# Reordering one slot of a fused attention loop: full-array products first, then both score groups, then values and denominators

## The chip, the cores and the metric

The kernel runs on one Trainium2 chip, the same program on each of its 8 cores, with different tokens on each and nothing exchanged between them. Each core has a matrix engine (TensorE, PE in the profile), a vector engine (VectorE, DVE), an activation engine (ScalarE, ACT), a general engine (GpSimd, POOL) that here only issues DMAs, and SyncE (SP), which issues the other DMAs. Each engine works through its own list of instructions in the order in which the program gives them, and stops at an instruction whose semaphores have not been reached. The metric is the device time of the slowest core in microseconds (us).

## The reference, cut to what matters

One transformer layer over 16 sequences of 2048 tokens with 1024 features; each core takes 2 sequences (4096 tokens).

```python
h = layernorm(x)
Q, K, V = h @ wq, h @ wk, h @ wv             # 16 heads of 64
local  = softmax over a window of 256 keys back (blocks of 256) @ V
remote = latent attention (64 pooled latents, 8 heads) @ r_out_w
gl = sigmoid(Q . gate_local_w); gr = sigmoid(Q . gate_remote_w)     # one number per token and head
x = x + (gl * local + gr * remote) @ w_out
h = layernorm(x)
for blk in range(3):                          # feed-forward, quantised weights with a low-rank part
    y = gelu(layernorm(qlora_linear(h, 2*blk)))
    h = qlora_linear(y, 2*blk + 1) + h
x = x + h
# qlora_linear: h @ ((q / 7.5 - 1) * scale + lb @ la).T + bias
```

## The kernel before, in words

A core's 4096 tokens are 8 tiles of 512 (`NJ = 8`, index `j`); a sequence is 4 tiles (`JS = 4`), so the first tile of a sequence (j = 0 and 4) has no keys behind it and has fewer score blocks. The program has three parts: a latent part (the remote attention, up to about 264 us of the span), the local attention loop (to about 855 us), and the feed-forward part.

The attention loop is software-pipelined over tiles. Of tile j it first computes the values projection and the gate logits, and then goes through 8 slots, p = 0..7, each for one pair of heads, numbered g = 8j + p. A slot holds work of several tiles: the attention of pair g, the k and q projections of tile j+1 (for j = 7, where there is no next tile, the first feed-forward product `y1` stands in their place), the output projection `wout` of tile j-2, and `bcast`, which spreads the softmax and gate factors of the pair of the tile before over the partitions. At p = 1 and 5 a slot also has `lora`, a product of the low-rank part for one chunk of dequantised feed-forward weights.

The products of a slot differ in how they use the 128x128 array. `project`, `wout` and `y1` are 8 matmuls of 128 rows by 128 columns, 512 elements wide (lines 543, 553, 571 and 441). `scores` (line 453) and `bcast` (line 530) work on 64 rows, two at a time. `attend` writes 32 columns, four at a time: values at line 483, denominators at line 496. `lora` (line 514) has 32 rows.

The order is written out by hand, once for each engine. In a slot TensorE does bcast, k, wout, (lora), attend(g), first and second scores of pair g+1, q, third scores of g+1. ScalarE follows the same order: evacuation of k (`k_evac`, line 810), of the attention values (line 960, into `A_O`), `exp_a` and `exp_b` (line 821, 1024 elements each), now and then `centre` (line 846), `exp_p(..., "sc")` (line 821), evacuation of q (line 752). VectorE does `spread` (lines 1159 and 1160, multiplying by the factors that bcast left), `mask_c(g)` (line 1114), `add_sides` (line 1166), `dequant_w` at p = 1 and 5 (lines 1211, 1219, 1230), `resid` on wout's result (line 1178), and `mask_ab(g+1)` (line 1114). For j = 1 `spread` stands behind `mask_c`.

All results pass through PSUM in units that are shared in turn; before a product overwrites a unit it waits until the last content has been read (`u.drained`):

- `S0` (two banks): first scores and third scores. The third scores wait for `exp_a`, the next first scores for the exponential of the third.
- `S1` (two banks): second scores, `bcast` and `lora`. bcast waits for `exp_b`; lora waits for `spread`; the second scores wait for whatever stood there last, at p = 1 and 5 `dequant_w`.
- `UO`, `UD`: attention values and denominators.
- `J[0]`, `J[1]`: k, wout and q (or y1), in turn.

attend(g) also waits for `p_masked`, the mask after the third exponential.

Of the kernel before, what the change touches and what calls it, by code (L numbers as in the profile page):

```python
# [85 lines left out]
def build_program():  # L86
# [38 lines left out]
    with contextlib.ExitStack() as es:  # L125
# [200 lines left out]
        def pe(t):  # L326
# [139 lines left out]
            def scores_b(g):  # L466
                scores(g, S1, "sb", ([(-1, 0, 2, 0)] if (g // 8) % JS else []) + [(2, 2, 2, 256)])

            def scores_c(g):
                scores(g, S0, "sc", [(1, 1, 3, 0), (3, 3, 1, 384)])  # L470
# [194 lines left out]
            for j in range(NJ):  # L665
                for n in range(8):
                    if j >= 1:
                        values(j, n)
                    if n == 3:
                        u = junit["z", j] = nextj()  # L670
                        k = u.take("z", j)
                        t.wait_ge(u.drained, k)
                        if j == 0:
                            for m in (6, 7):
                                w = junit["q", 0, m]
                                t.wait_ge(w.drained, w.nth["q", 0, m])
                        for c in range(8):
                            for side in range(2):
                                for qq in range(4):
                                    mm = t.matmul(u.ap[32 * qq:32 * qq + 32, side * 128:side * 128 + 128],  # L680
                                                  GZ[:, (2 * c + side) * 32:(2 * c + side) * 32 + 32],
                                                  a(A_Q + c * 512 + qq * 128, 128),
                                                  start=(c == 0 and side == 0), stop=(c == 7 and side == 1))
                        mm.then_inc(u.filled)
                if 1 <= j < NJ - 1:
                    t.wait_ge(ld_xt[(j + 1) % 2], 16 * ((j + 1) // 2))
                for p in range(8):
                    g = 8 * j + p
                    if j >= 1:
                        bcast(g - 8)  # L690
                    if j + 1 < NJ:
                        project("k", wk, j + 1, p)
                    else:
                        y1(p // 4, 2 * (p % 4))
                    if j >= 2:
                        wout(j - 2, p)
                    if p in (1, 5):
                        lora(2 * j + p // 4)
                    if p == 0:
                        for n in (6, 7):  # L700
                            u = junit["v", j, n]
                            t.wait_ge(u.drained, u.nth["v", j, n])
                    attend(g)
                    if g + 1 < 8 * NJ:
                        scores_a(g + 1)
                        scores_b(g + 1)
                    if j + 1 < NJ:
                        project("q", wq, j + 1, p)
                    else:
                        y1(p // 4, 2 * (p % 4) + 1)  # L710
                        if p == 5:
                            stats(0)
                    if g + 1 < 8 * NJ:
                        scores_c(g + 1)


            for oc in range(8):
# [31 lines left out]
        def act(s):  # L749
# [73 lines left out]
            def exp_a(g):  # L823
                exp_p(g, S0, "sa", 0, 0)
# [110 lines left out]
            for j in range(NJ):  # L935
# [9 lines left out]
                for p in range(8):  # L945
                    g = 8 * j + p
                    if p % 2 == 0 and 4 * (j - 2) + p // 2 - 1 >= 0:
                        rstd_a(4 * (j - 2) + p // 2 - 1)
                    if j + 1 < NJ:
                        k_evac(j + 1, p)  # L950
                    else:
                        if p == 0:
                            s.wait_ge(cb_done, 1)
                        if p == 6:
                            rstd_b(0)
                        y1_evac(p // 4, 2 * (p % 4))
                    if j >= 1:
                        s.wait_ge(mixed, g - 7)
                    s.wait_ge(UO.filled, UO.nth["av", g])
                    s.activation(a(A_O + p * 512, 512), UO.ap, AF.Identity).then_inc(UO.drained)  # L960
                    if g + 1 < 8 * NJ:
                        exp_a(g + 1)
                        exp_b(g + 1)
                    if p in (2, 6) and j < 4:
                        centre(2 * j + p // 4)
                    if g + 1 < 8 * NJ:
                        exp_p(g + 1, S0, "sc", 1024, 0)
                    if j + 1 < NJ:
                        evac(junit["q", j + 1, p], ("q", j + 1, p), a(A_Q + p * 512, 512))
                    else:  # L970
                        y1_evac(p // 4, 2 * (p % 4) + 1)
                    if j + 1 == NJ and p < 4:
                        square_s(0, 2 * p)
                        square_s(0, 2 * p + 1)
# [713 lines left out]
```

## Time and profile before

| | |
|---|---|
| median of 3 runs | 1600.84 us (1599.74, 1600.84, 1633.67) |
| profiled execution, its own time | 1590.74 us |
| span of its slowest core (core 0) | 1589.2 us |
| PE busy | 1487.5 us, 94% |
| DVE busy | 995.0 us, 63% |
| ACT busy | 878.9 us, 55% |
| attention loop | about 264 to 855 us of the span |

The profiled execution's time is 1.5 us more than its span. All times of the rows are counted from the start of the span of core 0. A row of the timeline gives the start, the length from the first start to the last end, the engine, the line, what is written from what, and how many instructions it merges; in square brackets stands the idle time of the engine just before and what ended it. Matmuls overlap, and their recorded ends are modelled, so distances between starts are what to go by. Where a group of 8 matmuls shows as x7, one record is missing; the row of the weight loads (PEld) has all 8 then.

### The profile page before, as it was taken

The numbers are of one execution on the slowest core, as the hardware profiler recorded it, in microseconds if no ns is written. First come the engines' busy times: TensorE is split into PE (matmuls) and PEld (weight loads), VectorE is DVE, ScalarE is ACT, GpSimd is POOL, SyncE is SP. The second block draws the span as 40 slices with busy tenths as digits, with TensorE's granted clock in tenths as the row PEclk, the third lists the DMA queues.
The fourth block names the chain that finished last, engine by engine and source line by source line (L and its number), as shares of the span: only waits on it lengthen the run. The fifth ranks groups of instructions, "written<-read, shape, count | busy, mean of one in ns | idle before, by whom it ended". The sixth has DMA issues, their size and how long they took to land.

```text
span 1589.2 us, 30285 instructions; the slowest of 8 cores (1573.7 to 1589.2 us)
## 1 busy us (share of the span) xinstructions
PE 1487.5 (94%) x10737; PEld 691.1 (43%) x10906; DVE 995.0 (63%) x1549; ACT 878.9 (55%) x1274; POOL 110.5 (7%) x196
## 2 busy tenths in 40 slices
PE   4797999988999999999998989999999999999997
PEld 2443443444444444444444334444444444444443
DVE  6874313335656565757575766787776767766765
ACT  3575566756555554656576355565556544554552
POOL 3220000000000000000001000011001010000000
PEclk9898999999999999999999999999999999999999
DMA  9999416311223242423756455323122222223323
GB/s 133 178 195 204 99 53 132 93 55 35 78 71 100 68 121 68 115 60 100 143 126 113 86 123 100 80 69 88 34 40 51 50 51 46 87 80 120 120 80 126
DMA packets 100113, 149.82 MB, mean 94 GB/s; under 512 B 46928, under 2 KB 58752, under 8 KB 97280
## 3 DMA queue, kind: packets, MB, share of 16 engines
q0 software_dynamic: 34352, 64.51, 22.2%
q1 hardware_dynamic: 65616, 83.38, 18.1%
q8 instruction: 91, 1.49, 0.4%
q14 instruction: 54, 0.44, 0.1%
HBM read 122.60 MB, written 49.81 MB: 108 GB/s over the span
## 4 chain that ended last, share of the span: by engine, by line
PE 76%; DVE 6%; DMA 6%; issue 5%; ACT 4%; DVEq 2%; POOL 0%; ACTq 0%; POOLq 0%; SPq 0%
PE ps L571 20%; PE ps L601 12%; PE ps L441 10%; PE ps L553 7%; PE ps L606 7%; PE ps L543 6%; DMA AR<-x_in 5%; PE ps L453 3%; PE ps L483 2%; PE ps L364 2%; ACT AR L821 2%; DVEq L1264 1%; PE ps L584 1%; PE ps L496 1%; PE ps L609 1%
## 5 line engine op out<-in xcount | busy, mean ns | idle before, releaser
L441 PE MATMUL ps<-XT,WA 128*128 128x512 bf16 x964 | 229.8, 381 | 9.4 <-issue 8.8
L571 PE MATMUL ps<-WA,WB 128*128 128x512 bf16 x999 | 226.2, 379 | 8.8 <-DVE AR L1178 3.9
L821 ACT ACTIVATE AR<-ps 128x1024 bf16<-128x1024 f32 (+2 forms) x192 | 179.4, 969 | 43.1 <-PE ps L453 40.6
L874 ACT ACTIVATE AR<-AR,LNB,LNG 128x512 bf16<-128x512 bf16 x176 | 134.0, 806 | 124.2 <-DVE AR L1297 124.2
L853 ACT ACTIVATE AR<-ps,CB 128x512 bf16<-128x512 f32 x176 | 118.4, 684 | 146.6 <-PE ps L571 146.5
L1114 DVE TENSOR_TENSOR AR<-AR,MLOC 128x768 bf16<-128x768 bf16 (+2 forms) x144 | 116.6, 820 | 103.5 <-ACT AR L821 100.6
L571 PEld LDWEIGHTS ps<-WA,WB 128*128 128x128 bf16 x1024 | 97.4, 98 | 126.8 <-issue 15.0
L441 PEld LDWEIGHTS ps<-XT,WA 128*128 128x128 bf16 x1024 | 91.2, 98 | 119.7 <-issue 25.7
L1314 DVE SCALAR_TENSOR_TENSOR WA<-ps,BIAS,WA 128x512 bf16<-128x512 f32 x128 | 95.6, 748 | 51.2 <-PE ps L601 49.2
L606 PE MATMUL ps<-XT,AR 128*128 128x512 bf16 x496 | 121.8, 384 | 5.2 <-ACT AR L874 4.2
L543 PE MATMUL ps<-WA,AR 128*128 128x512 bf16 x504 | 120.4, 379 | 2.2 <-ACT AR L853 0.9
L1286 DVE TENSOR_TENSOR AR<-AR 128x512 bf16<-128x512 bf16 x160 | 66.6, 423 | 84.0 <-ACT AR L853 80.9
L1297 DVE TENSOR_TENSOR AR<-AR 128x512 bf16<-128x512 bf16 x176 | 113.4, 683 | 3.2 <-issue 2.9
L571 PE MATMUL ps<-WA,AR 128*128 128x512 bf16 x500 | 113.6, 379 | 0.7 <-issue 0.2
L553 PE MATMUL ps<-WA,XT 128*128 128x512 bf16 x504 | 112.7, 379 | 1.6 <-issue 1.1
L601 PE MATMUL ps<-AR 128*128 128x512 bf16 x501 | 112.7, 379 | 0.6
L1159 DVE TENSOR_TENSOR AR<-ps,AR 128x512 bf16<-128x512 f32 x64 | 43.8, 684 | 101.0 <-PE ps L530 101.0
L960 ACT ACTIVATE AR<-ps 128x512 bf16<-128x512 f32 x64 | 38.2, 597 | 106.9 <-PE ps L483 101.0
L601 PE MATMUL ps<-AR,XT 128*128 128x512 bf16 x376 | 86.9, 385 | 3.0 <-ACT AR L874 2.6
L543 PEld LDWEIGHTS ps<-WA,AR 128*128 128x128 bf16 x512 | 48.8, 98 | 63.5 <-issue 13.1
L882 ACT ACTIVATE AR<-ps 128x512 bf16<-128x512 f32 x64 | 38.1, 597 | 69.1 <-PE ps L553 69.1
L601 PEld LDWEIGHTS ps<-AR 128*128 128x128 bf16 x512 | 50.0, 98 | 60.6 <-issue 2.3
(168 smaller groups left out, 1981.7 us busy)
## 6 DMA issues: line engine op xcount, KB each, us to landing
AR<-scT POOLq DMA_DIRECT2D x48, 512.0 KB, 7.4
y<-AR SPq DMA_DIRECT2D x32, 512.0 KB, 2.9
AR<-x_in POOLq DMA_DIRECT2D x63, 256.0 KB, 9.2
remT<-AR SPq DMA_DIRECT2D x8, 1024.0 KB, 6.9
AR<-remT SPq DMA_DIRECT2D x64, 128.0 KB, 3.9
xn<-AR SPq DMA_DIRECT2D x32, 256.0 KB, 3.2
AR<-x SPq DMA_DIRECT2D x32, 256.0 KB, 3.3
x<-AR SPq DMA_DIRECT2D x31, 256.0 KB, 3.5
```

Source lines behind the costliest of these rows:

```text
L441: mm = t.matmul(u.ap, w(c, p * 128, 128), xt(j % 2, c), start=(c == 0), stop=(c == 7))
L543: mm = t.matmul(u.ap, a(A_MIX + (j % 2) * 4096 + c * 512 + sub * 128, 128), wo(c, hf * 512, 512), start=(c == 0), stop=(c == 7))
L553: mm = t.matmul(u.ap, xt(j % 2, c, tc * 128, 128), wv(c, hf * 512, 512), start=(c == 0), stop=(c == 7))
L571: mm = t.matmul(u.ap, wmat(2 * k3, c, oc * 128, 128), rt(tt, c), start=(c == 0), stop=(c == 7))
L601: mm = t.matmul(u.ap, wmat(2 * k3 + 1, c, oc * 128, 128), ybuf(s, c * 512, 512), start=(c == 0), stop=(c == 7))
L606: t.matmul(u.ap, ybuf(s, c * 512 + sub * 128, 128), wmat(5, c, hf * 512, 512), start=(c == 0), stop=False)
L821: s.activation(dst[:, :, col + lo:col + hi], src[:, :, lo:hi], AF.Exp, scale=ISQ).then_inc(u.drained)
L853: s.activation(ybuf(sn, oc * 512, 512), u.ap, AF.Identity, bias=CB[:, 8 * i + oc:8 * i + oc + 1]).then_inc(u.drained)
L874: s.activation(yb, yb, AF.Gelu, bias=LNB[:, 8 * i + c:8 * i + c + 1], scale=LNG[:, 8 * i + c:8 * i + c + 1]).then_inc(g_done)
L1114: op = v.tensor_tensor(p3[:, :, lo:hi], p3[:, :, lo:hi], m3, op=ALU.mult)
L1297: v.tensor_tensor(yb, yb, rsbuf(sn), op=ALU.mult).then_inc(yn_done)
L1314: v.scalar_tensor_tensor(rt(tt, oc), u.ap, BIAS[:, 8 * i1 + oc:8 * i1 + oc + 1], rt(tt, oc), op0=ALU.add, op1=ALU.add).then_inc(u.drained)
```

## The change

Nothing is computed differently; the same instructions stand in another order in a slot. On TensorE the q projection (or y1) moves up behind wout and lora, the first and second scores of g+1 follow, then attend(g), then the third scores, and then bcast of the next slot's pair. Only the bcast of p = 0 keeps its place ahead of k. On ScalarE `centre` and the evacuation of q move ahead of exp_a and exp_b, and the evacuation of the attention values stands behind them. VectorE, GpSimd and SyncE are untouched.

```diff
@@ TensorE
                 for p in range(8):
                     g = 8 * j + p
-                    if j >= 1:
+                    if j >= 1 and p == 0:
                         bcast(g - 8)
                     if j + 1 < NJ:
                         project("k", wk, j + 1, p)
@@
-                    attend(g)
-                    if g + 1 < 8 * NJ:
-                        scores_a(g + 1)
-                        scores_b(g + 1)
                     if j + 1 < NJ:
                         project("q", wq, j + 1, p)
                     else:
                         y1(p // 4, 2 * (p % 4) + 1)
                         if p == 5:
                             stats(0)
                     if g + 1 < 8 * NJ:
+                        scores_a(g + 1)
+                        scores_b(g + 1)
+                    attend(g)
+                    if g + 1 < 8 * NJ:
                         scores_c(g + 1)
+                    if j >= 1 and p < 7:
+                        bcast(g - 7)
@@ ScalarE
+                    if p in (2, 6) and j < 4:
+                        centre(2 * j + p // 4)
+                    if j + 1 < NJ:
+                        evac(junit["q", j + 1, p], ("q", j + 1, p), a(A_Q + p * 512, 512))
+                    else:
+                        y1_evac(p // 4, 2 * (p % 4) + 1)
+                    if g + 1 < 8 * NJ:
+                        exp_a(g + 1)
+                        exp_b(g + 1)
                     if j >= 1:
                         s.wait_ge(mixed, g - 7)
                     s.wait_ge(UO.filled, UO.nth["av", g])
                     s.activation(a(A_O + p * 512, 512), UO.ap, AF.Identity).then_inc(UO.drained)
                     if g + 1 < 8 * NJ:
-                        exp_a(g + 1)
-                        exp_b(g + 1)
-                    if p in (2, 6) and j < 4:
-                        centre(2 * j + p // 4)
-                    if g + 1 < 8 * NJ:
                         exp_p(g + 1, S0, "sc", 1024, 0)
-                    if j + 1 < NJ:
-                        evac(junit["q", j + 1, p], ("q", j + 1, p), a(A_Q + p * 512, 512))
-                    else:
-                        y1_evac(p // 4, 2 * (p % 4) + 1)
```

TensorE before, in one slot of tile j = 2, from the values of attend(g) to the output projection of the next slot. `d_J0`, `d_J1`, `d_S0`, `d_S1`, `d_O` are the drained semaphores of the units above; line 441 is a projection, 543 wout, 483 and 496 attend, 453 scores, 530 bcast.

```order
L483 MATMUL ps<-AR 32x256 [waits p_masked,d_O]
...
L496 MATMUL ps<-AR,OHD 32x128 x24
L453 MATMUL ps<-AR 128x384 [waits d_J1,d_J0,d_S0]
...
L453 MATMUL ps<-AR 128x256 [waits d_S1]
L453 MATMUL ps<-AR 128x256 x3
L441 MATMUL ps<-XT,WA 128x512 [waits d_J1]
L441 MATMUL ps<-XT,WA 128x512 x7
L453 MATMUL ps<-AR 128x384 [waits d_S0]
...
L530 MATMUL ps<-AR,SEL 128x256 [waits d_S1]
```

A whole projection (the two rows of line 441) stands between the scores that fill S0 and S1 and the two products that need S0 and S1 empty again. The same place in the changed kernel, from the q projection on:

```order
L441 MATMUL ps<-XT,WA 128x512 [waits d_J1]
L441 MATMUL ps<-XT,WA 128x512 x7
L453 MATMUL ps<-AR 128x384 [waits d_J1,d_J0,d_S0]
...
L453 MATMUL ps<-AR 128x256 [waits d_S1]
L453 MATMUL ps<-AR 128x256 x3
L483 MATMUL ps<-AR 32x256 [waits p_masked,d_O]
...
L496 MATMUL ps<-AR,OHD 32x128 x24
L453 MATMUL ps<-AR 128x384 [waits d_S0]
...
L530 MATMUL ps<-AR,SEL 128x256 [waits d_S1]
```

Now attend(g) stands there in its place, and the projection comes ahead of the first scores.

ScalarE before, one slot of the same tile (810 evacuates k, 960 the attention values, 752 q; 821 is an exponential; `f_...` are the filled semaphores):

```order
L810 ACTIVATE AR<-ps 128x512 [waits f_J1]
L960 ACTIVATE AR<-ps 128x512 [waits mixed,f_O]
L821 ACTIVATE AR<-ps 128x2x512 [waits f_S0]
L821 ACTIVATE AR<-ps 128x2x512 [waits f_S1]
L821 ACTIVATE AR<-ps 128x2x512 [waits f_S0]
L752 ACTIVATE AR<-ps 128x512 [waits f_J0]
```

And in the changed kernel, where the same functions stand two to eleven lines lower in the file (812, 754, 823, 971):

```order
L812 ACTIVATE AR<-ps 128x512 [waits f_J1]
L754 ACTIVATE AR<-ps 128x512 [waits f_J0]
L823 ACTIVATE AR<-ps 128x2x512 [waits f_S0]
L823 ACTIVATE AR<-ps 128x2x512 [waits f_S1]
L971 ACTIVATE AR<-ps 128x512 [waits mixed,f_O]
L823 ACTIVATE AR<-ps 128x2x512 [waits f_S0]
```

The evacuation of q now stands directly ahead of the two exponentials, and that of the attention values between them and the third.

## Rows read from the trace of the kernel before

**Rows 1.** The page: busy time of each engine.

```profile
PE 1487.5 (94%) x10737; PEld 691.1 (43%) x10906; DVE 995.0 (63%) x1549; ACT 878.9 (55%) x1274; POOL 110.5 (7%) x196
```

**Rows 2.** Length, busy us (PE, PEld, DVE, ACT, POOL), TensorE clock, DMA: tiles 1, 7.

```profile
328.42:385.68 57.26, 49.11 (x637) 23.32 (x645) 33.46 (x50) 37.26 (x49) 2.38 (x4) 0.97 0.20 58
...
788.76:854.94 66.18, 61.56 (x696) 29.36 (x705) 46.73 (x70) 42.91 (x65) 5.19 (x10) 1.00 0.49 115
```

**Rows 3.** Timeline, all engines: slot p = 0 of tile 5.

```profile
633.09 0.39 PE L530 MATMUL ps<-AR,SEL 64*128 64x256 bf16 x4
...
633.41 1.90 PE L441 MATMUL ps<-XT,WA 128*128 128x512 bf16 x8
...
635.15 1.89 PE L543 MATMUL ps<-WA,AR 128*128 128x512 bf16 x7
635.41 0.60 ACT L810 ACTIVATE AR<-ps 128x512 bf16<-128x512 f32 x1 [1.11 <-PE ps L441]
...
636.97 0.84 PE L483 MATMUL ps<-AR 128*32 128x256 bf16 x24
...
637.63 0.51 PE L496 MATMUL ps<-AR,OHD 128*32 128x128 bf16 x24
...
638.08 0.61 PE L453 MATMUL ps<-AR 64*128 64x384 bf16 x8
638.57 1.94 ACT L821 ACTIVATE AR<-ps 128x1024 bf16<-128x1024 f32 x2
638.61 1.41 PEld L441 LDWEIGHTS ps<-XT,WA 128*128 128x128 bf16 x8 [0.21 <-issue]
...
640.45 0.39 PE L453 MATMUL ps<-AR 64*128 64x384 bf16 x4
...
640.68 0.38 PE L530 MATMUL ps<-AR,SEL 64*128 64x256 bf16 x4
```

**Rows 4.** Timeline, tile 1: an evacuation and two exponentials on ACT, and waits of PE.

```profile
348.10 0.60 ACT L960 ACTIVATE AR<-ps 128x512 bf16<-128x512 f32 x1 [1.04 <-DVE AR L1166]
...
348.59 1.93 ACT L821 ACTIVATE AR<-ps 128x1024 bf16<-128x1024 f32 x2
...
350.67 0.39 PE L530 MATMUL ps<-AR,SEL 64*128 64x256 bf16 x4 [0.31 <-ACT AR L821]
...
353.52 0.84 PE L483 MATMUL ps<-AR 128*32 128x256 bf16 x24 [0.62 <-DVE AR L1114]
```

**Rows 5.** Timeline: the slot with lora of tile 5, p = 1, from lora to the next bcast.

```profile
644.55 0.39 PE L514 MATMUL ps<-LALB 32*128 32x512 bf16 x2
...
645.44 1.22 DVE L1219 SCALAR_TENSOR_TENSOR AR<-AR,ps 128x1024 bf16<-128x1024 f32 x1 [0.16 <-issue]
...
646.81 0.39 PE L453 MATMUL ps<-AR 64*128 64x256 bf16 x4 [0.29 <-DVE AR L1219]
...
649.20 0.38 PE L530 MATMUL ps<-AR,SEL 64*128 64x256 bf16 x4
```

**Rows 6.** Timeline, tile 4 (first of a sequence): the exponentials, and PE's two bcasts around slot p = 3.

```profile
563.23 1.30 ACT L821 ACTIVATE AR<-ps 128x768 bf16<-128x768 f32 x2
...
580.55 0.38 PE L530 MATMUL ps<-AR,SEL 64*128 64x256 bf16 x4
...
587.81 0.38 PE L530 MATMUL ps<-AR,SEL 64*128 64x256 bf16 x4
```

**Rows 7.** Waits of PE in the attention loop: us in total, times, longest us.

```profile
PE ps L483 <- DVE AR L1114: 2.9, 7, 0.6
...
PE ps L543 <- ACT AR L752: 0.8, 4, 0.2
```

**Rows 8.** Timeline of PE, tile 1: lora, and the projection behind it.

```profile
338.52 0.39 PE L514 MATMUL ps<-LALB 32*128 32x512 bf16 x2 [2.02 <-DVE AR L1160]
...
341.39 2.60 PE L441 MATMUL ps<-XT,WA 128*128 128x512 bf16 x7 [0.34 <-issue]
```

**Rows 9.** Timeline of PE, tile 7: the product behind the statistics.

```profile
839.88 1.89 PE L571 MATMUL ps<-WA,WB 128*128 128x512 bf16 x8 [1.63 <-ACT WA L853]
```

## The prediction

> **What bounds the kernel now.** I read the page first: TensorE is busy for 94% of the span and no other engine for more than 63% [rows 1]. The reader should take from it that time is lost or won only where TensorE's own sequence gets longer or shorter. Next come the stretches of the loop. In tile 1 the clock is 0.97 and PE is idle for 8 of 57.26 us; in tile 7 it is idle for under 5 of 66.18 us [rows 2]. Tiles 2 to 6 are as full as tile 7. So this loop is TensorE-bound with few waits, and the gain to be had is small from the start.
>
> The timeline then gives the anatomy of an ordinary slot, by distances between starts [rows 3]: bcast to k 0.32 us, k to wout 1.74, wout to values 1.82, values to denominators 0.66, denominators to scores 0.45, first and second scores 0.53 up to the first weight load of q at 638.61, q to third scores 1.84, third scores to bcast 0.23. The sum is 7.59 us, the distance from bcast to bcast (633.09 to 640.68). A product of 8 full matmuls takes 1.74 when another full product follows (k to wout) and 1.82 to 1.84 when another shape follows, so a change of shape costs some 0.1 us.
>
> ScalarE matters for what it releases. Four distances are needed. An evacuation begins 2.00 us after the start of its product (633.41 to 635.41). An exponential can begin 0.49 us after its scores start (638.08 to 638.57) [rows 3]. Behind an evacuation of 0.60 us that is still running the next exponential begins 0.49 us after the evacuation's start, and two exponentials of 1024 last 1.93 us; PE starts 0.15 us after the second has ended (348.59 + 1.93 = 350.52, bcast at 350.67) [rows 4].
>
> **The change: what an ordinary slot becomes.** I count from the start of the first scores of g+1. Ahead of them now stands q, which started 1.84 us earlier. The scores need 0.53 us, values 0.66, denominators 0.45 [rows 3], so TensorE could start the third scores at 1.64 us, and bcast 0.23 later.
>
> They need S0 and S1 empty. ScalarE starts the evacuation of q at 2.00 - 1.84 = 0.16 us, and only 0.49 later, at 0.65, exp_a. This is 0.16 later than the scores alone would allow. The pair takes 1.93 us [rows 4], so exp_b ends at 2.58; exp_a ends at about 1.67 (half of the pair and a little for their overlap). With the 0.15 us of release the third scores start at 1.82, after a wait of 0.18, and bcast at 2.73 where it could have started at 2.05: a wait of 0.68. In the old order the q projection, 1.84 us, stood between the scores and these two products and covered the same two exponentials; now attend(g), 1.11 us, stands there. That is the cover the change gives away.
>
> The new slot is 2.73 + 0.32 (bcast) + 1.74 (k) + 1.74 (wout) + 1.84 (q) = 8.37 us against 7.59, so **0.78 us more**. There are 7 such slots (p = 0 to 6) in each of tiles 2, 3, 5, 6 and 7: 35 x 0.78 = +27.3 us.
>
> In tile 4, the first of a sequence, scores and exponentials are shorter. The pair takes 1.30 us there, and the old slot 7.26 (580.55 to 587.81) [rows 6]. The pair ends at 0.65 + 1.30 = 1.95, bcast starts at 2.10, the slot is 2.10 + 5.64 = 7.74: 7 x 0.48 = +3.4.
>
> At p = 7 no bcast follows, and only the wait of 0.18 for exp_a counts, against one change of shape less (0.1): 5 x 0.08 = +0.4.
>
> **Waits that go.** (1) The second scores of a slot with lora wait for dequant_w on VectorE. Such a slot took 8.52 us (640.68 to 649.20), 0.93 over the ordinary one [rows 3, 5]. lora itself lasts to 645.02 or so, 0.46 us. Now q's 1.84 us stand between lora and the scores in place of 1.11 us of attend; VectorE, which began dequant_w 0.89 us after lora and took 1.22 [rows 5], would be done at 2.11 + 0.15 = 2.26 after lora, and the second scores come at 0.46 + 1.84 + 0.22 = 2.52. So 0.47 goes in each of 12 such slots of tiles 2 to 7, one of which waited 0.35 longer: -6.0. (2) wout waits in four slots for q's evacuation behind centre [rows 7]: -0.8. (3) In tile 7 the product behind the statistics waited 1.63 for q's late evacuation [rows 9]. That wait goes. Next in line there are two smaller ones: the statistics then take the J unit that wout left, whose reader on VectorE now stands behind dequant_w (some 0.8 us late), and the y1 after them waits for ScalarE's reciprocal root (some 0.4). Together -0.4. y1's evacuation is some 0.09 us longer than q's: +0.6. (4) At the end of the loop the first product of the next stage waits less for its unit, and ScalarE starts the next evacuations later in exchange: -0.4.
>
> **Tiles 0 and 1.** Tile 0 has no bcast. Its values waited for the mask of the third exponential, as did two pairs of tile 1, 2.9 us in all [rows 7]; four products now stand before them, so that wait goes. The third scores now wait for exp_a instead, about 0.28, and one change of shape is saved. With the lora waits I get -1.6 us for the tile. In tile 1 there is no wout. Its five ordinary slots become 0.32 + 1.74 + 1.84 + 2.73 = 6.63 us. At p = 1 and 5 lora waits for a spread that stands behind mask_c. The third exponential ends no earlier than before, since the evacuation of the values now stands ahead of it, so the wait stays near 2.0 us [rows 8], and such a slot is 9.3 us. Five of 6.63, two of 9.3, and 6.0 at p = 7 are 57.8 against 57.3 [rows 2]: +0.5.
>
> **Edits at nothing.** bcast(g-7) at the end of a slot rather than at the start of the next is the same place on TensorE. centre (a little over 1 us) ahead of q's evacuation is hidden, because wout's 1.74 us and q's lie between the end of k's evacuation and the start of q's. If that cover were gone (tile 0 has no wout) it would still fit by 0.1 us. The evacuation of the values, later by about two exponentials, is waited for only by attend of the next slot, over 6 us on. Its own wait (`mixed`) is long met. The third exponential ends at about 4.0 us, its mask at 5.8, and attend(g+1) asks for it at 8.9. VectorE, GpSimd and SyncE keep their order, and no transfer is on their way that gets nearer to its use.
>
> **Sum.** 27.3 + 3.4 + 0.4 - 6.0 - 0.8 - 0.4 + 0.6 - 0.4 - 1.6 + 0.5 = +23.0 us. The profiled execution, 1590.74 us (1589.2 of span and 1.5 around it), becomes 1613.7. The median of the runs shown was 10 us above the profiled execution, and I add the same difference there: 1600.84 + 23 = **1624 us**, 1.4% slower.
>
> **Bounds.** What I have not seen is a change straight from 64-row to 32-column matmuls. It may cost nothing or 0.2 us like two changes, but it hardly matters: in the slots with bcast, ScalarE's chain sets the time, and PE merely waits less by as much. Only p = 7 and tile 0 keep such a difference, 15 x 0.1, so 1.5 us to either side. exp_a could start at 0.49 if q's evacuation got done earlier; then 49 slots (7 in each of tiles 1 to 7) are shorter by 0.16: -8. It could also start 0.60 after the evacuation's start rather than 0.49, if it doesn't overlap with it: +5. Lora's waits may stay in part, if VectorE comes late: +3 at most of the 6.
>
> **Rivals.**
> *The waits don't appear (3%).* S1 would have to be empty when TensorE gets to bcast. The order of ScalarE and the durations speak against it, as does the row in which bcast waited 0.31 us even behind a whole projection [rows 4]. Then the change keeps its savings: 0.1 us in some 60 slots (6), the lora waits (6), and the small ones (3): 1600.84 - 15 = 1586.
> The Trainium skill, TensorEngine Tiling (Array Packing), Key Properties, says that changing the tiling mode, not just the tile, drains the engine. By that rule the change should win, since a slot has one change of mode less (four instead of five). The trace shows the price of it as 0.08 to 0.1 us [rows 3], which gives this rival's 6 us and no more.
> *The clock falls (8%).* This is the case of slower by over 2%. After lora's wait of 2.02 us in tile 1 seven matmuls took 2.60 us instead of 1.67, that is about 0.93 us lost in one product, and the granted clock of the tile is 0.97 [rows 2, 8]. If the new waits, 0.86 us in every slot, did this once a slot in the 42 slots of tiles 2 to 7, it would be +39 on top of 23: 1663 us. It decides as soon as one slot in four is hit, as 2% is 32 us. Against it: tile 1 had waits of 0.31 and 0.62 us within 3 us of each other [rows 4], and 1.63 us once in tile 7, and the eight matmuls after this one took 1.89, which is the full-speed length [rows 9].
> The Trainium skill, TensorE: Matmul & The Clock Gate, section on a second HAM failure mode (psum-queue depth-cycling), tells of frequent short idles between groups of matmuls that made the clock go down and up again. No row here shows it for waits under 2 us; it is the reason why this rival has 8% and not 2.
> *ScalarE is worse than worked out (6%).* If VectorE's or ScalarE's work slips so that the chain of a slot is 0.25 us longer still, 49 slots add 12: 1636.
>
> **How the numbers follow.** The forecast as worked out has 83%. The likeliest time is 1624. Its own bounds are 1624 - 8 - 1.5 and 1624 + 5 + 3, and some 4 us to either side for the scatter of runs (two of the three shown differ by 1.1, and the profiled one lies 10 under them): 1610 to 1636. I let the upper end reach a little into the rivals of the slow side: 1609 to 1639. Two per cent, about what a measurement of this kernel can tell from no change, is 1633 on the slow side and 1569 on the fast. The first rival, too, is within 2%. Slower by over 2%: the clock's 8%, two thirds of the third rival, and 2% from the edge of the forecast, together 13%. Faster by over 2%: 2%. Within 2%: 85%.
>
> **What would show it.** In the profile after, line 532 (bcast) has waits for the exponential (line 823) of some 0.7 us in about 49 slots, the third scores shorter ones of 0.1 to 0.2; a slot of tile 5 is 8.4 us from bcast to bcast. ScalarE has q's evacuation, then two exponentials without a gap. lora slots of tiles 2 to 7 show no wait for dequant_w; the wait of 1.63 us in tile 7 is gone. The feed-forward part is unchanged. I am wrong if bcast waits little (then exp_b ended sooner than 2.6 us after the scores' start), or if groups of eight matmuls at twice the usual spacing stand after the waits (the clock).

## The result, and the profile after

The changed kernel took 1623.8 us (median of 5 runs) beside 1599.7 us for the kernel before (5 runs). The ratio is 1.0145, with a 95% interval of 1.0132 to 1.0159: 1.4% slower, within 2%, and at the predicted 1624 us. Two of the five executions after and one of the five before were slow ones, in which the cores of a die show a lower granted clock; the ratio is of the others. The profiled execution took 1622.62 us, its span 1621.1 us (core 2).

I read the page first: the busy time of each engine, and the costliest group of ScalarE.

```profile
PE 1530.8 (94%) x10906; PEld 702.8 (43%) x10906; DVE 994.4 (61%) x1549; ACT 868.6 (54%) x1274; POOL 110.4 (7%) x196
...
L823 ACT ACTIVATE AR<-ps 128x1024 bf16<-128x1024 f32 (+2 forms) x192 | 181.2, 982 | 2.6 <-PE ps L453 2.4
```

The same group on the page of the kernel before (line 821 there):

```profile
L821 ACT ACTIVATE AR<-ps 128x1024 bf16<-128x1024 f32 (+2 forms) x192 | 179.4, 969 | 43.1 <-PE ps L453 40.6
```

PE has the share of [rows 1], 94%, although the kernel is slower: busy shares say nothing here. The exponential (line 823) now waits for only 2.6 us in the whole program, where it waited for 43.1 us. ScalarE is no longer the engine that waits for the scores; TensorE waits for it.

The waits of PE in the attention loop, with total, count and longest in us:

```profile
PE ps L530 <- ACT AR L823: 21.6, 42, 0.5
PE ps L453 <- ACT AR L823: 5.5, 21, 1.1
PE ps L514 <- DVE AR L1162: 4.1, 2, 2.0
PE ps L584 <- DVE AR L1180: 0.9, 1, 0.9
PE ps L364 <- DVE AR L1083: 0.7, 1, 0.7
PE ps L453 <- DVE AR L1213: 0.2, 1, 0.2
PE ps L543 <- ACT AR L867: 0.2, 1, 0.2
```

bcast (line 530) waits for the exponential 42 times. Before, it did so four times, all in tile 1:

```profile
PE ps L530 <- ACT AR L821: 1.1, 4, 0.3
```

The 42 are seven in each of tiles 1, 2, 3, 5, 6 and 7. In tile 4 bcast comes 0.48 us after the third scores where 0.23 is enough, so it waits 0.25 us there too, which is not recorded as idle time. The waits of values for the mask and of wout for q's evacuation [rows 7] are gone; one wait of wout, 0.2 us for another evacuation, stands in tile 7.

The timeline, PE and ACT, of slot p = 0 of tile 5, the one of [rows 3]; it begins at bcast, 653.11:

```profile
655.43 0.60 ACT L812 ACTIVATE AR<-ps 128x512 bf16<-128x512 f32 x1 [1.10 <-PE ps L441]
...
656.90 1.89 PE L441 MATMUL ps<-XT,WA 128*128 128x512 bf16 x8
...
658.72 0.61 PE L453 MATMUL ps<-AR 64*128 64x384 bf16 x8
658.89 0.60 ACT L754 ACTIVATE AR<-ps 128x512 bf16<-128x512 f32 x1 [2.86 <-PE ps L441]
...
659.26 0.84 PE L483 MATMUL ps<-AR 128*32 128x256 bf16 x24
659.38 1.94 ACT L823 ACTIVATE AR<-ps 128x1024 bf16<-128x1024 f32 x2
...
659.93 0.51 PE L496 MATMUL ps<-AR,OHD 128*32 128x128 bf16 x24
...
660.54 0.40 PE L453 MATMUL ps<-AR 64*128 64x384 bf16 x4
...
661.46 0.39 PE L530 MATMUL ps<-AR,SEL 64*128 64x256 bf16 x4 [0.52 <-ACT AR L823]
```

Counted from the first scores, 658.72: q's evacuation begins at 0.17, the exponentials at 0.66 and end at 2.60, the third scores come at 1.82 and bcast at 2.74. The slot is 661.46 - 653.11 = 8.35 us against 7.59. The wait of bcast is recorded as 0.52; by starts it is larger: the third scores are followed by bcast after 0.92 us where 0.23 is enough [rows 3], so 0.69. The recorded idle time is measured from a modelled end.

The stretches of tiles 1, 2 and 7 (length, then busy time of PE, PEld, DVE, ACT and POOL, TensorE's granted clock, DMA share, GB/s):

```profile
336.38:396.50 60.12, 51.96 (x646) 24.07 (x645) 31.59 (x48) 36.39 (x49) 2.38 (x4) 0.94 0.21 58
411.53:478.59 67.06, 62.65 (x710) 29.56 (x709) 44.90 (x72) 37.40 (x55) 3.93 (x7) 1.00 0.34 87
...
817.30:886.81 69.51, 63.62 (x706) 29.86 (x705) 44.90 (x67) 41.01 (x64) 2.77 (x5) 1.00 0.49 109
```

Tiles 1 and 7 answer to [rows 2]: 60.12 and 69.51 us against 57.26 and 66.18. The clock is 1.00 in tiles 2 to 7 in spite of the waits.

From the first scores to the first product of the feed-forward part the attention loop took 613.7 us against 591.3 (263.59 to 854.94 before, 273.08 to 886.81 after): +22.4. What follows it took 734.3 us in both. The spans of the two profiled executions differ by 31.9 us; the 9.5 us that are missing here lie ahead of the loop, in code that the change doesn't touch. The same stretch of two cores of the one execution of the changed kernel, core 2 and then core 0:

```profile
100.00:200.00 100.00, 99.65 (x464) 45.10 (x463) 42.36 (x54) 61.75 (x96) 0.94 (x1) 0.81 0.81 161
```

```profile
100.00:200.00 100.00, 94.19 (x489) 43.61 (x497) 44.57 (x58) 67.79 (x108) 0.94 (x1) 0.98 0.81 170
```

Core 2 was granted a clock of 0.81 there and did 464 matmuls, core 0 had 0.98 and did 489. Cores 2 to 7 had 0.81 all, core 1 had 1.00, and their spans are 1617 to 1621 us against 1598 and 1602 for cores 0 and 1. Therefore the experiments are also compared by the loop alone: from the start of the first mask on VectorE (line 1114 or 1116) to the start of the last. This distance is 582.5 to 585.3 us on the cores of the kernel before (I use 584) and 605.2 to 607.3 after (606), whatever the core's clock ahead of it.

### The profile page after: what moved, and what is told of

Same layout as the page of the kernel before. It is cut to its first block, busy times and chain, and to the rows that moved or that the text cites. A ratio compares the mean times of both kernels' runs of the same rounds, so it can differ in the third digit from the quotient of the medians.

```text
span 1621.1 us, 30454 instructions; the slowest of 8 cores (1597.5 to 1621.1 us)
## 1 busy us (share of the span) xinstructions
PE 1530.8 (94%) x10906; PEld 702.8 (43%) x10906; DVE 994.4 (61%) x1549; ACT 868.6 (54%) x1274; POOL 110.4 (7%) x196
## 4 chain that ended last, share of the span: by engine, by line
PE 84%; ACT 5%; issue 3%; DMA 3%; DVE 3%; DVEq 1%; POOL 1%; ACTq 0%; POOLq 0%; SPq 0%
PE ps L571 19%; PE ps L441 14%; PE ps L601 13%; PE ps L553 7%; PE ps L543 7%; PE ps L606 7%; PE ps L364 4%; ACT AR L823 4%; PE ps L453 2%; PE ps L380 2%; PE ps L483 2%; DMA AR<-sell 2%; PE ps L530 1%; DMA AR<-x_in 1%; PE ps L584 1%
## 5 line engine op out<-in xcount | busy, mean ns | idle before, releaser
L441 PE MATMUL ps<-XT,WA 128*128 128x512 bf16 x1024 | 247.8, 390 | 0.0
L441 PEld LDWEIGHTS ps<-XT,WA 128*128 128x128 bf16 x1024 | 96.3, 100 | 125.3 <-issue 37.2
L754 ACT ACTIVATE AR<-ps 128x512 bf16<-128x512 f32 x72 | 42.9, 597 | 151.2 <-PE ps L441 144.5
L553 PEld LDWEIGHTS ps<-WA,XT 128*128 128x128 bf16 x512 | 49.3, 99 | 61.0 <-issue 7.2
```

Source lines behind the costliest of these rows:

```text
L441: mm = t.matmul(u.ap, w(c, p * 128, 128), xt(j % 2, c), start=(c == 0), stop=(c == 7))
L553: mm = t.matmul(u.ap, xt(j % 2, c, tc * 128, 128), wv(c, hf * 512, 512), start=(c == 0), stop=(c == 7))
```

## The experiments

All ratios are against the kernel before, run on the same chip in the same job. "Loop" is the distance just described, in us.

| kernel | ratio (95%) | loop | slot |
|---|---|---|---|
| before | 1 | 584 | 7.59 |
| the change | 1.0145 (1.0132 to 1.0159) | 606 | 8.35 |
| the change again | 1.0143 (1.0125 to 1.0160) | 606 | 8.35 |
| 1 exponentials ahead of q's evacuation | 1.0081 (1.0057 to 1.0106) | 597.6 | 8.19 |
| 2 bcast behind k | 1.0041 (1.0027 to 1.0055) | 591.5 | 7.87 |
| 3 values' evacuation first | 1.0781 (1.0760 to 1.0803) | 707.5 | 9.68 |
| 4 wout as cover | 1.0098 (1.0081 to 1.0115) | 600.3 | 7.58 |
| 5 before, lora ahead of wout | 1.0054 (1.0037 to 1.0071) | 594.8 | |
| 6 = 4, spread first in tile 1 | 1.0087 (1.0067 to 1.0107) | 599.8 | |
| 7 the change, spread first in tile 1 | 1.0113 (1.0091 to 1.0134) | 603.3 | |
| 8 = 6, dequant_t early | 0.9992 (0.9974 to 1.0009) | 580.6 | |
| 9 before, dequant_t early | 0.9977 (0.9965 to 0.9989) | 577.8 | |

### 1. The exponentials ahead of q's evacuation

If ScalarE's chain sets the slot, the 0.16 us that q's evacuation takes out of it can be had back by order alone.

```diff
@@ the change, ScalarE
                         centre(2 * j + p // 4)
+                    if g + 1 < 8 * NJ:
+                        exp_a(g + 1)
+                        exp_b(g + 1)
                     if j + 1 < NJ:
@@
-                    if g + 1 < 8 * NJ:
-                        exp_a(g + 1)
-                        exp_b(g + 1)
                     if j >= 1:
```

> The changed kernel, with exp_a and exp_b ahead of the evacuation of q on ScalarE. Theory A (the time of a slot is set by ScalarE's chain from q's evacuation over exp_a and exp_b to bcast): exp_a starts 0.49 us after the first scores instead of 0.65, bcast at 2.57 instead of 2.74, so 49 slots are 0.16 us shorter: about -8 us against the changed kernel, near 1615 us. Rival B (what costs is on TensorE: the direct step from 64-row to 32-column matmuls, or the shape changes): no change, 1623 us.

Two bcasts in the timeline of PE, a slot apart, in tile 5:

```profile
663.85 0.40 PE L530 MATMUL ps<-AR,SEL 64*128 64x256 bf16 x4 [0.52 <-ACT AR L823]
...
672.03 0.40 PE L530 MATMUL ps<-AR,SEL 64*128 64x256 bf16 x4 [0.52 <-ACT AR L823]
```

8.18 us where it was 8.35, and a loop shorter by 8.4 us: the prediction's bound of -8 for this case. TensorE's products are the same, in the same order, so the slot's length comes from ScalarE's chain and not from TensorE's changes of shape.

### 2. bcast behind k

This gives the wait something to be hidden behind: k of the next slot needs neither S0 nor S1.

```diff
@@ the change, TensorE
-                    if j >= 1 and p == 0:
-                        bcast(g - 8)
                     if j + 1 < NJ:
                         project("k", wk, j + 1, p)
@@
+                    if j >= 1:
+                        bcast(g - 8)
                     if j >= 2:
                         wout(j - 2, p)
@@
-                    if j >= 1 and p < 7:
-                        bcast(g - 7)
```

> The changed kernel, with bcast behind the k projection of the next slot, so that k's 1.74 us cover exp_b. Theory A: the wait of bcast for exp_b (0.69 us in a slot) goes, two changes of shape come (0.2 us), the third scores still wait 0.17 for exp_a; a slot of tile 5 goes from 8.35 to about 7.87 us; in all about -20 us, near 1603 us. Rival B: a slot gets longer by the two changes of shape, 8.55 us, +10 us, 1633 us.

PE's timeline, the same k product of two slots and the bcast between, and PE's largest wait in the loop:

```profile
659.04 1.67 PE L441 MATMUL ps<-XT,WA 128*128 128x512 bf16 x7 [0.16 <-issue]
660.65 0.39 PE L530 MATMUL ps<-AR,SEL 64*128 64x256 bf16 x4
...
666.91 0.59 PE L441 MATMUL ps<-XT,WA 128*128 128x512 bf16 x2 [0.16 <-issue]
```

```profile
PE ps L514 <- DVE AR L1160: 7.2, 12, 2.6
```

bcast waits no more, and the slot is 7.87 us. The loop won 14.5 us (15.6 by TensorE alone, from the first scores to the last values) and not 20. Part of the rest went into a new wait: `spread` on VectorE starts later with bcast, and lora, which needs S1 empty, waits for it, 0.2 us in each of ten slots of tiles 2, 3 and 5 to 7 (such a slot is now 0.69 us longer than the others, not 0.43) and 2.63 instead of 2.04 in the two of tile 1. Another part is tile 4: bcast waited only 0.25 us there, little more than the 0.2 expected for the two new changes of shape, and its slot went from 7.71 to 7.65.

### 3. The values' evacuation ahead of the exponentials

This makes the waits larger, to see whether the clock would fall: the change's order on TensorE, with ScalarE evacuating the values before it starts exp_a.

```diff
@@ the change, ScalarE
-                    if g + 1 < 8 * NJ:
-                        exp_a(g + 1)
-                        exp_b(g + 1)
                     if j >= 1:
                         s.wait_ge(mixed, g - 7)
@@ (the evacuation of the values)
+                    if g + 1 < 8 * NJ:
+                        exp_a(g + 1)
+                        exp_b(g + 1)
```

> The changed kernel, with ScalarE's evacuation of the attention values put back ahead of exp_a and exp_b. Theory A: exp_a can only start behind the evacuation of values that TensorE produces after the scores, at 1.98 us after the scores' start instead of 0.65; third scores at 3.15 and bcast at 4.06 us instead of 2.74; a slot of tile 5 is 9.7 us, and the whole +78 us, near 1702 us. If waits of 2 us at one place in each slot bring the clock down, still longer. Rival B: TensorE's shapes are the same, 1623 us.

PE's timeline behind a pair of waits, and a slot without that effect:

```profile
767.91 0.40 PE L453 MATMUL ps<-AR 64*128 64x384 bf16 x4 [1.43 <-ACT AR L823]
768.83 0.61 PE L530 MATMUL ps<-AR,SEL 64*128 64x256 bf16 x4 [0.52 <-ACT AR L823]
769.37 3.23 PE L441 MATMUL ps<-XT,WA 128*128 128x512 bf16 x8
...
779.13 0.40 PE L453 MATMUL ps<-AR 64*128 64x384 bf16 x4 [1.43 <-ACT AR L823]
...
788.81 0.39 PE L453 MATMUL ps<-AR 64*128 64x384 bf16 x4 [1.43 <-ACT AR L823]
```

An ordinary slot is 9.68 us, as worked out, and yet the loop grew by 101.5 us (94.6 to 103.2 on the single cores) and not by 78. The projection at 769.37 took 3.23 us where its neighbours take 1.90, and the granted clock from its start to 773.00 was 0.62 of full speed: most of this stretch ran at the lower level of 1.2 GHz. Two of the stretches that make up this loop (granted clock behind POOL's column):

```profile
330.00:450.00 120.00, 101.55 (x1055) 45.23 (x1052) 46.22 (x70) 53.76 (x76) 2.38 (x4) 0.90 0.14 41
...
860.00:980.00 120.00, 100.08 (x1024) 45.93 (x1021) 61.23 (x92) 59.25 (x91) 4.46 (x8) 0.96 0.42 96
```

So some 24 us of this kernel's loss are the clock's, an estimate by subtraction of the expected from the measured. The rival "the clock falls" is real, but not with the waits of the change: 0.18 and 0.69 us in a slot left the clock at 1.00 in tiles 2 to 7; with 1.43 and 0.69 (recorded 0.52) it fell in some slots and not in others. The Trainium skill, TensorE: Matmul & The Clock Gate, section on a second HAM failure mode, describes short idles between groups of matmuls that make the clock go down and up; these rows agree for the larger waits, and tiles 2 to 7 of the changed kernel show that it needn't happen with the smaller.

### 4. wout as cover

Here the old property is restored in the new order: a full product between the second scores and attend.

```diff
@@ the change, TensorE
-                    if j >= 2:
-                        wout(j - 2, p)
                     if p in (1, 5):
                         lora(2 * j + p // 4)
@@
                         scores_b(g + 1)
+                    if j >= 2:
+                        wout(j - 2, p)
                     attend(g)
```

> The changed kernel, with wout moved from between k and q to between the second scores and attend: one full projection again lies between the scores and the products that need S0 and S1 back, and one change of shape more per slot. Theory A: no wait of bcast or third scores in tiles 2 to 7, a slot of tile 5 is 7.59 us as before the change, and the lora waits stay away: about -29 us against the changed kernel, near 1595 us, slightly under the kernel before. Tiles 0 and 1 have no wout and stay as in the changed kernel. Rival B: 1628 us or more.

Two bcasts of PE's timeline, and then the waits of PE:

```profile
658.80 0.38 PE L530 MATMUL ps<-AR,SEL 64*128 64x256 bf16 x4
...
666.38 0.38 PE L530 MATMUL ps<-AR,SEL 64*128 64x256 bf16 x4
```

```profile
PE ps L514 <- DVE AR L1162: 24.6, 14, 2.0
...
PE ps L571 <- ACT AR L867: 2.1, 1, 2.1
```

The slot is 7.58 us without a wait, as before the change: cover is all that was missing. But of 29 us only 5.7 came. lora stands directly behind k now, and waits some 1.7 us in each of the 12 slots of tiles 2 to 7 (the other two are the waits of 2.04 us in tile 1, as in the changed kernel). Such a slot takes 9.92 us, 2.33 over the others where it was 0.43 over: 12 x 1.9 = 23 us, which is all that is missing. What it waits for is on VectorE, whose timeline shows it; lora starts at 652.81:

```profile
649.12 1.21 DVE L1116 TENSOR_TENSOR AR<-AR,MLOC 128x2048 bf16<-128x2048 bf16 x1
650.24 1.22 DVE L1202 SCALAR_TENSOR_TENSOR AR<-AR 128x1024 f32<-128x1024 int8 x1
651.38 0.69 DVE L1161 TENSOR_TENSOR AR<-ps,AR 128x512 bf16<-128x512 f32 x1
651.98 0.68 DVE L1162 TENSOR_TENSOR AR<-ps,AR 128x512 bf16<-128x512 f32 x1
```

The mask of the first two exponentials and `dequant_t` (line 1202) stand ahead of the two multiplications of spread.

### 5. The kernel before, with lora ahead of wout

Meant to win back the waits for dequant_w alone, in the old order.

```diff
@@ before, TensorE
-                    if j >= 2:
-                        wout(j - 2, p)
                     if p in (1, 5):
                         lora(2 * j + p // 4)
+                    if j >= 2:
+                        wout(j - 2, p)
```

> The kernel before, with lora ahead of wout in its slot. Tests the term of the prediction that counts 0.5 us for the second scores' wait for dequant_w in each of 12 slots of tiles 2 to 7. If it is right, wout's 1.74 us cover dequant_w, the waits of line 453 for dequant_w are gone in tiles 2 to 7, a lora slot of tile 5 goes from 8.52 to about 8.05 us, and the whole is 6 us faster than before, near 1594 us. Rival: VectorE gets to dequant_w no earlier, since the spread and the masks stand ahead of it, and the wait stays: 1600 us.

A miss, with the wrong sign: the loop is 10.8 us longer. The waits for dequant_w did go in tiles 2 to 7, and this one came, 1.42 us each there (0.56 in tile 4):

```profile
PE ps L514 <- DVE AR L1160: 19.4, 14, 2.0
```

It is the same wait as in experiment 4, without the change. wout had been lora's cover.

### 6 and 7. spread ahead of mask_c in tile 1

```diff
@@ VectorE, on top of 4 and of the change
-                    if j >= 2:
+                    if j >= 1:
                         spread(g - 8)
                     mask_c(g)
-                    if j == 1:
-                        spread(g - 8)
```

> The version with wout as cover (between second scores and attend) and, in tile 1 too, VectorE's spread ahead of mask_c, as in the later tiles. Expected: the 29 us of the wout cover, and the two waits of 2.04 us of lora in tile 1 with the slow matmuls behind them (10.6 us slots become 7.1): 7 us more. Near 1587 us, 0.8% faster than the kernel before. Rival: mask_c later makes attend wait in tile 1, and 3 us of the 7 come back.

> The changed kernel, with VectorE's spread ahead of mask_c in tile 1. Tests where the 2.9 us of tile 1 come from, for which the prediction had 0.5. If from the waits of 2.04 us of lora for the spread and the half-speed matmuls that follow, both go: tile 1 from 60.1 to about 53 us, the whole -7 us, near 1616 us. If TensorE's slow matmuls there have another cause, the waits go and the slow matmuls stay: -4 us.

In the changed kernel it brought 2.7 us of 7. On the cores profiled tile 1 became shorter by 3.9 us, 56.26 against 60.12; over all eight cores it is 56.3 against 58.9 on the mean, which is about the loop's difference. In the kernel with wout as cover it brought only 0.5 us in the loop. Tile 1 went from 58.9 to 56.3 us there too, but on six of the eight cores the slot p = 1 of tile 4 took some 11.25 us and not 9.76 (in experiment 4 on one): the matmuls behind lora's wait of 1.90 us were slow in it (granted clock 0.59 from 572.00 to 576.00 on core 1). On the other two cores the loop is 596.7 us. Why the cores differ is open. lora in tile 1, and what follows it, first in the changed kernel and then in experiment 7:

```profile
347.27 0.39 PE L514 MATMUL ps<-LALB 32*128 32x512 bf16 x2 [2.04 <-DVE AR L1162]
347.59 3.29 PE L441 MATMUL ps<-XT,WA 128*128 128x512 bf16 x8
350.81 0.85 PE L453 MATMUL ps<-AR 64*128 64x384 bf16 x8
```

```profile
338.03 0.39 PE L514 MATMUL ps<-LALB 32*128 32x512 bf16 x2 [1.43 <-DVE AR L1162]
338.36 1.90 PE L441 MATMUL ps<-XT,WA 128*128 128x512 bf16 x8
```

A wait of 2.04 us is followed by a slow projection, 3.29 us, and slow scores. After a wait of 1.43 us the same projection takes 1.90.

The granted clock from 347.27 to 351.60 in the changed kernel was 0.61. Two such slots, 8.56 us each where they were 10.60 and 10.36, are the 3.9 us: 0.6 us of wait in each, and some 1.3 us of slow matmuls. The slow matmuls do not always come: each core has two waits of 2.04 us in tile 1, and over the eight cores of this execution and of experiment 10's slow matmuls stood behind 16 of the 32; otherwise the slot takes 9.16 us. Behind the 16 waits of 1.43 and 1.44 us of experiment 7 there were none.

### 8 and 9. dequant_t early

If the chain on VectorE is what lora waits for, `dequant_t`, which needs nothing from the slot, has to go ahead of it: in 8 (on top of 6) ahead of `resid`, in 9 (the kernel before and nothing else) ahead of mask_ab.

```diff
@@ 8, VectorE, on top of 6
                         dequant_w(2 * j + p // 4)
+                    if p in (0, 4):
+                        dequant_t(2 * j + p // 4)
@@
                         mask_ab(g + 1)
-                    if p in (0, 4):
-                        dequant_t(2 * j + p // 4)
@@ 9, VectorE, in the kernel before
-                    if g + 1 < 8 * NJ:
-                        mask_ab(g + 1)
                     if p in (0, 4):
                         dequant_t(2 * j + p // 4)
+                    if g + 1 < 8 * NJ:
+                        mask_ab(g + 1)
```

> The version with wout as cover and spread first in tile 1, and dequant_t moved from behind mask_ab to ahead of resid on VectorE, where VectorE is idle for 3 us. In the version without this step lora, then directly behind k, waited 1.71 us for the spread in each of 12 slots, since mask_ab (1.23) and dequant_t (1.22) stood ahead of the spread. If that chain is the cause, the wait falls to about 0.5 us, tile 1's two waits to about 0.4 with no slow matmuls behind: about -20 us against that version, 0.997 of the kernel before. Rival: the waits of lora come from something else on VectorE (wout's residual) and stay over 1 us: 1.007.

> The kernel before, with dequant_t ahead of mask_ab on VectorE instead of behind it. In the slot with lora VectorE then reaches dequant_w 0.35 us sooner, and the second scores' wait of 0.3 us goes; in tile 1 mask_c, spread and lora come 0.8 us sooner and the slow matmuls behind lora's wait may go. Together -7 us, 0.9955 of the kernel before. Rival: dequant_t waits for its load there, and holds up mask_ab: no gain or a loss.

The waits of PE in the loop, of 8 and then of 9:

```profile
PE ps L514 <- DVE AR L1162: 7.2, 14, 0.6
PE ps L530 <- ACT AR L823: 3.7, 7, 0.5
```

```profile
PE ps L483 <- DVE AR L1114: 4.6, 8, 1.6
...
PE ps L514 <- DVE AR L1160: 2.1, 2, 1.2
```

In 8, lora waits 0.6 us and not 2.0, and the loop is 19.7 us shorter than in 4: VectorE's order was the cause. This is the changed order with its cover restored and the next wait in line made shorter, and it is as fast as the kernel before, with a ratio not told from 1. In 9 the loop won 6.2 us of 7. More than half of it, 3.5 us on the mean of the cores, is tile 1, where lora's waits fell to 1.21 and 0.90 us and no core has slow matmuls. The rival named for it shows in part: once, in tile 0 of the core profiled, `dequant_t` waits for its load (VectorE idle for 4.7 us), the mask behind it comes late, and values wait 1.6 us. Five of the eight cores don't have this wait. The ratio of 9 is the lowest of all, 0.23% under the kernel before, and the interval excludes 1.

### 10. The change again

> The changed kernel once more, unaltered. In the first measurement six of the profiled cores had a granted clock of 0.81 in the latent part (100 to 200 us), where nothing was changed, against 0.95 to 1.00 in the profile of the kernel before. If the slowdown is all in the attention loop, it is again 1.014 with whatever clock the latent part has, and first to last mask of the loop 606 us against 584. If the latent part's clock contributed to the first ratio, it comes out smaller, near 1.012 or less, when both kernels have the same clock there.

This asks whether the 9.5 us ahead of the loop belong to the change. In both kernels the cores with a mean clock of about 0.975 had the long spans and those of about 0.99 the short ones: 1591 to 1599 us and 1573 to 1587 before, 1614 to 1621 and 1593 to 1607 with the change. The change costs some 22 us on either sort. In the profiled execution four cores had a clock of 0.81 from 100 to 200 us, and their first mask starts at 270 to 275 us; the other four had 0.95 to 0.98, and theirs starts at 255 to 262. The loop is 606 us on both sorts (604.4 to 606.1). So the 9.5 us come from which cores have which clock ahead of the loop.

## Why the prediction was right

**Time and mechanism.** The forecast of +23.0 us stands against +22.4 in the loop and against 24 between the medians. ScalarE's chain of a slot came out as worked out: third scores at 1.82 us (1.82), bcast at 2.74 (2.73), slot 8.35 (8.37). Experiment 1 took the piece of 0.16 out and got 8 us; experiments 2 and 4 put a full product ahead of bcast (in 4 of the third scores too), and its wait was gone in the slots shown.

**The sum by tiles.** I sort the terms of the sum by tile, from its own parts, and put the measured lengths beside them:

| tile | forecast | measured |
|---|---|---|
| 0 | -1.6 | -1.4 |
| 1 | +0.5 | +2.9 |
| 2, 3 | +3.9, +4.2 | +3.3, +3.6 |
| 4 | +2.5 | +2.6 |
| 5, 6 | +4.6, +4.6 | +4.3, +4.4 |
| 7 | +4.4 | +3.3 |
| sum | 23.1 | 22.9 |

(23.1 for 23.0 is rounding. The products between two tiles are 0.09 us shorter each time, 15.03 for 15.12, which makes 22.9 the 22.4 of the loop.) The sum is better than its terms, since misses cancel.

**Tile 1, mis-sized: +2.9 us for +0.5.** The five slots without lora (6.62 us for 6.63) and the wait of 2.04 us were right. A slot with lora takes 9.16 us, forecast 9.3, if no slow matmuls follow its wait; on the core profiled they followed twice, and the two slots took 10.6 and 10.4. From the start of q to attend the changed kernel took 347.59 to 351.60, 4.01 us, where 1.84 + 0.53 would be full speed, 1.6 us lost. The forecast left these slow matmuls out of the changed tile, although the tile that it is set against, 57.3 us, has one such slot [rows 2, 8]: 9.86 us, where cores without slow matmuls took 8.55. So the term compares unlike cases. With no slow matmuls at all tile 1 is 57.47 us after (core 7 of experiment 10) and 55.95 before (cores 4 and 6), +1.5. They came behind 9 of 16 such waits before and 16 of 32 after, and the means over the eight cores are 57.5 us before and 58.9 and 58.7 after, +1.3. The rest of the +2.9 is which core was the slowest in each execution.

**wout's waits, mis-sized: -1.4 for -0.8.** I took the recorded 0.2 us each [rows 7]. By starts the slot before was 7.93 us there against 7.59, so 0.34 each. This is the same understatement as with bcast, and it is 0.3 us in tile 2 and 0.3 in tile 3.

**The end of the loop, mis-sized: -1.1 for -0.3** (the forecast's -0.4, and 0.1 for p = 7). The last slot went from 7.80 to 6.72 us, since the wait of 0.93 for the unit of the first product behind the loop is gone whole. That is most of tile 7's difference. Its other terms held: 0.88 us for VectorE's late reader (forecast 0.8), a slot with 0.36 too much for the reciprocal root (0.4).

**lora's waits, right.** Slots with lora take 8.78 us in tiles 2, 3, 5 and 6, 0.43 over the others, and were 0.93 over (tile 4: 0.42, and 0.8 to 0.9 before). But I named only dequant_w as what lora's slots wait for. Experiments 4 and 5 showed how near the next wait was: put lora one product earlier and it waits 1.4 to 1.7 us for spread.

**The rivals.** "The waits don't appear" is excluded by the 42 waits and by experiment 1. The Trainium skill, TensorEngine Tiling (Array Packing), Key Properties, has a change of tiling mode drain the engine, so that one change less should be a gain. The trace agrees that a change costs time: a product ahead of another shape takes 1.82 us and not 1.74 here too. But the one change less lies between the first scores and bcast, where TensorE waits for ScalarE anyway, and so it gains nothing. "The clock falls" didn't occur in tiles 2 to 7, with a granted clock of 1.00 in each; in experiment 3, with waits of 1.43 and 0.69 us in a slot, it did. "ScalarE is worse" didn't occur: the ordinary slots of tile 2 are all 8.34 or 8.35 us. Two slips in the text of the prediction change nothing in this: its chances of slower by over 2% add up to 14% and not 13, and bcast stands in line 530 of the changed kernel, not 532.

**What was right by luck.** The profiled execution before was 10 us under its median, and I added this difference without a reason for it. The forecast for the profiled execution itself, 1613.7 us, is 9 us short of the measured 1622.6; these are the 9.5 us ahead of the loop, and the added 10 us stood in for them. Experiment 10 shows cores some 15 us apart in both kernels by their clock ahead of the loop; the difference can be had from that. It was not shown for the very runs of the median.

**Not tried.** k of the next slot between attend and the third scores would cover both waits, but by the program's buffers (three blocks of 256 keys for each pair, used in turn) it overwrites keys that the scores still read. It would need another buffer.

## What to carry to other kernels

Before you move a product, ask what it covers: the full product between the one that fills a PSUM unit and the one that reuses it paid for ScalarE's reading, and moving it away cost 0.76 us a slot. Work the slot out from the reader's chain as well as from TensorE's, and take waits by distances between starts, not by the recorded idle time. When a wait is removed, look at the order on the engine behind it: here lora's cover, and `dequant_t` ahead of `spread` on VectorE, decided whether 29 us of gain became 5.7 or 25. And when slow matmuls come and go, compare a stretch on all the cores, not on the slowest of each kernel.

## What the runs showed that was not expected

- In one execution of one program the granted clock of a dense stretch (PE busy 99.65 of 100 us on core 2) was 0.81 on six cores and 0.98 and 1.00 on the two others, which were some 18 us faster in the end. In the kernel before, too, cores with a mean clock of 0.975 and of 0.99 stood apart within one execution, by some 14 us on the mean (experiment 10).
- Waits of 0.18 and 0.69 us in every slot of 8.35 us never lowered the clock in tiles 2 to 7. Waits of 1.43 and 0.69 us in a slot of 9.7 us did so some of the time (3.23 us for a product of 1.90). The waits of 2.04 us in tile 1, two on each core, did so in half of the cases, 16 of 32, with the same instructions around them (3.29 us for 1.90 in the one shown); those of 1.43 us in the same place did so in none of 16.
